# Scores of the later 128 queries as three float32r products of two-part operands, with the low part of g made by VectorE

## The reference

```python
q = (x @ Wq).reshape(b, t, h, e).transpose(0, 2, 1, 3)
k = (x @ Wk).reshape(b, t, h, e).transpose(0, 2, 1, 3)
v = (x @ Wv).reshape(b, t, h, e).transpose(0, 2, 1, 3)
q = q / math.sqrt(e)
dot = jnp.einsum('bhqe,bhke->bhqk', q, k)
dot = jnp.where(causal[None, None], dot, -jnp.inf)
att = jax.nn.softmax(dot, axis=-1)
out = jnp.einsum('bhqk,bhke->bhqe', att, v)
out = out.transpose(0, 2, 1, 3).reshape(b, t, h * e)
return out @ Wo + bo
```

## Time and profile before

| | us |
|---|---|
| median of three runs (2622.41 to 2632.78) | 2631.57 |
| span of the profiled execution, first to last instruction | 2620.5 |
| TensorE busy in it | 2267.1 (87%) |
| VectorE busy | 1887.6 (72%) |
| ScalarE busy | 1689.2 (64%) |
| GpSimd busy | 1152.6 (44%) |
| first head with an expert unit beside it, to last head of the attention | 1574 to 2464 |

### The profile page before, as it was taken

One profiled execution on the slowest core, in us unless ns is written; L12 is line 12 of the kernel. 1 busy time (PEld: TensorE's weight loads), 2 busy tenths in 40 slices (PEclk: granted clock), 3 DMA queues, 4 the chain that ended last, 5 costly groups with the idle time before them and its releaser, 6 DMA issues.

```text
span 2620.5 us, 58544 instructions
## 1 busy us (share of the span) xinstructions
PE 2267.1 (87%) x16671; PEld 2017.4 (77%) x16687; DVE 1887.6 (72%) x8724; ACT 1689.2 (64%) x5272; POOL 1152.6 (44%) x1358
## 2 busy tenths in 40 slices
PE   4999787676666699999999999999999999999954
PEld 3887665455555588888888889999999999999854
DVE  4887757544443488888888887787788888888622
ACT  3787653222222477777777778888888778888643
POOL 6444100788888202222222224444444666456553
PEclk9999989777777899999999999999999999999987
DMA  2333200344444521110101016556554777387687
GB/s 81 101 100 88 82 22 1 66 74 74 78 75 74 101 62 34 32 34 29 36 28 36 28 55 167 155 157 161 152 155 128 223 214 224 109 233 208 173 254 234
DMA packets 304256, 283.95 MB, mean 108 GB/s; under 512 B 33932, under 2 KB 252652, under 8 KB 303937
## 3 DMA queue, kind: packets, MB, share of 16 engines
q1 hardware_dynamic: 254144, 211.15, 29.4%
q0 software_dynamic: 46336, 61.16, 10.2%
q10 hardware_dynamic: 3456, 7.89, 1.0%
HBM read 185.85 MB, written 88.43 MB: 105 GB/s over the span
## 4 chain that ended last, share of the span: by engine, by line
PE 54%; DVE 18%; POOL 14%; issue 8%; DMA 3%; SPq 1%; ACT 1%; ACTq 0%; DVEq 0%; POOLq 0%
POOL hbuf L828 8%; PE bank L2040 6%; PE bank L2127 6%; PE bank L2113 5%; PE bank L2048 5%; PE bank L2080 4%; PE bank L2088 4%; POOL xe L820 4%; PE bank L2039 3%; PE bank L2062 3%; PE bank L2060 3%; PE bank L2061 3%; DVE pr_place L1558 2%; DVE nmax L1540 2%; DVE pr_place L1548 2%
## 5 line engine op out<-in xcount | busy, mean ns | idle before, releaser
L862 POOL DMA_INDIRECT spread_rows<-kb,pos x256 | 248.6, 971 | 595.4 <-ACT pr_place L1072 468.9
L877 POOL DMA_INDIRECT zbuf<-pc,kb x248 | 247.9, 1000 | 258.2 <-DVE pc L1720 207.5
L1070 ACT ACTIVATE pr_place<-bank,nmax 128x128 f32<-128x128 f32 x512 | 188.8, 369 | 201.5 <-DVE nmax L1540 198.5
L2040 PE MATMUL bank<-xT,gT 128*128 128x256 f32 x1024 | 306.7, 381 | 0.0
L2048 PE MATMUL bank<-ident,pr_place 128*128 128x128 f32 x1536 | 254.3, 275 | 43.4 <-DVE pr_place L1558 43.1
L2048 PEld LDWEIGHTS bank<-ident,pr_place 128*128 128x128 f32 x1536 | 189.6, 140 | 127.4 <-DVE pr_place L1551 62.4
L1558 DVE COPY pr_place<-bank 128x384 f32<-128x384 f32 x512 | 281.5, 550 | 1.1 <-PE bank L2048 1.0
L1539 DVE TENSOR_REDUCE nmax<-bank 128x1 f32<-128x128 f32 x512 | 144.1, 281 | 175.3 <-PE bank L2040 172.3
L2127 PE MATMUL bank<-wvo_part,x_part 128*128 128x512 f32 x768 | 269.0, 458 | 0.0
L1080 ACT ACTIVATE bank<-causal 128x384 f32<-128x384 f32 x512 | 253.4, 495 | 19.8 <-PE bank L2171 3.6
L2113 PE MATMUL bank<-x_part,wqk_part 128*128 128x256 f32 x1536 | 245.6, 296 | 1.2 <-DVE x_part L1665 1.2
(11 more groups left out here) (334 smaller groups left out, 6233.6 us busy)
## 6 DMA issues: line engine op xcount, KB each, us to landing
pa<-bundle SPq DMA_DIRECT2D x198, 321.0 KB
wu_more<-bundle SPq DMA_DIRECT2D x66, 321.0 KB
junk<-zbuf SPq DMA_DIRECT2D x32, 512.0 KB
kb<-spread_rows SPq DMA_DIRECT2D x248, 65.0 KB
xrow<-xr SPq DMA_DIRECT2D x32, 320.0 KB, 2.4
hbuf<-h SPq DMA_DIRECT2D x32, 256.0 KB, 3.1
hx<-hbuf SPq DMA_DIRECT2D x64, 128.0 KB
h3buf<-h SPq DMA_DIRECT2D x64, 128.0 KB
```

The source lines that it names most:

```text
L2040: pe.matmul(s2[:, P:3 * P], g[:, P:2 * P], xT3[:, p], start=False, stop=True, skip_group_check=True)\
```

## The change

For blocks n of at least SPLIT_FROM = 14 * 2 + 4 = 32, the L2040 product (float32, later 128 queries against 256 keys) becomes three float32r products, with g as two parts in the new buffer g_part and x as the two parts that x_part already holds. ACT's copy of a pair of heads is made in two: the later halves into g_part as the rounded part, the earlier halves into gT. DVE subtracts the rounded part from the bank to make the low part and signals g_low. PE waits for g_low before the three products, and before the gate's transposes and products that write the same bank. The earlier 128 queries' product (L2039) stays float32. The buffer xe moves to memory that layer 1 reuses, so that g_part fits.

```diff
--- before.py
+++ after.py
@@ -210,7 +210,6 @@
         cnt4 = sb("cnt4", [P, TG])
         idx = sb("idx", [P, 4, TG], U32)
 
-        xe = sb("xe", [P, 2, TG, ROW])
         xeT = sb("xeT", [P, TG * P])
         wup = sb("wup", [P, 2, FF])
         bup_n = sb("bup_n", [8, FF])
@@ -322,9 +321,11 @@
             wkn = sbe("wkn", [P, H1 * C])
             wvn = sbe("wvn", [P, H1 * C])
             won = sbe("won", [P, H1, C])
+            xe = sbe("xe", [P, 2, TG, ROW])
         wqk_part = [sb(f"wqk_part{k}", [P, H1, C], F32R) for k in range(2)]
         wvo_part = [sb(f"wvo_part{k}", [P, H1, C], F32R) for k in range(2)]
         x_part = [sb(f"x_part{k}", [P, 2, 2 * P], F32R) for k in range(2)]
+        g_part = sb("g_part", [P, 2, 2, 2, P], F32R)
 
         w_in = sem("w_in")
         consts = sem("consts")
@@ -411,6 +412,7 @@
         parts_split = sem("parts_split")
         g_mm = sem("g_mm")
         g_ready = sem("g_ready")
+        g_low = sem("g_low")
         vo_mm = sem("vo_mm")
         vo_ready = sem("vo_ready")
         s_mm = sem("s_mm")
@@ -431,6 +433,12 @@
 
         def there(u, count=NB * H1):
             return not isinstance(u, int) or 0 <= u < count
+
+        SPLIT_FROM = PORTS[0][1] * 2 + 4
+
+        def late_half(h):
+            v = bank[GBANK][:, :].rearrange("p (k q) -> p k q", k=2)[:, :, P:2 * P]
+            return v, g_part[:, h // 2 % 2]
 
         consts4 = sem("consts4")
         b1_ready = sem("b1_ready")
@@ -1137,7 +1145,13 @@
                             gates_turned(i - 1)
                         if h % 2 == 0 and n < NB:
                             act.wait_ge(g_mm, 4 * n + h // 2 + 1)
-                            act.activation(gT[:, h // 2 % 2], bank[GBANK][:, :], ACT.Copy).then_inc(g_ready, 1)
+                            if n < SPLIT_FROM:
+                                act.activation(gT[:, h // 2 % 2], bank[GBANK][:, :], ACT.Copy).then_inc(g_ready, 1)
+                            else:
+                                late, parts = late_half(h)
+                                act.activation(parts[:, 0], late, ACT.Copy)
+                                act.activation(gT[:, h // 2 % 2].rearrange("p (k q) -> p k q", k=2)[:, :, 0:P],
+                                               bank[GBANK][:, :].rearrange("p (k q) -> p k q", k=2)[:, :, 0:P], ACT.Copy).then_inc(g_ready, 1)
                         if h < 4 and n < NB:
                             act.wait_ge(vo_mm, 4 * n + h + 1)
                             act.activation(vo[:, p, h % 2, (h // 2) * 512:(h // 2 + 1) * 512], bank[VBANK][:, :], ACT.Copy)\
@@ -1765,6 +1779,10 @@
                         if there(u - N_LAG):
                             norm_rest(u - N_LAG, (h - N_LAG) % H1)
                         root_step()
+                        if h % 2 == 0 and SPLIT_FROM <= n < NB:
+                            late, parts = late_half(h)
+                            dve.wait_ge(g_ready, 4 * n + h // 2 + 1)
+                            dve.tensor_tensor(parts[:, 1], late, parts[:, 0].bitcast(F32), ALU.subtract).then_inc(g_low, 1)
                         if there(u - T_LAG):
                             turn(u - T_LAG, (h - T_LAG) % H1)
                         root_step()
@@ -2037,6 +2055,13 @@
                 pe.wait_ge(g_ready, 4 * n + h // 2 + 1)
                 pe.wait_ge(mask_set, u + 1)
                 pe.matmul(s2[:, 0:P], g[:, 0:P], xT3[:, p, 0:P], start=False, stop=True, skip_group_check=True)
+                if n >= SPLIT_FROM:
+                    pe.wait_ge(g_low, 4 * (n - SPLIT_FROM) + h // 2 + 1)
+                    for m, (a, b) in enumerate(PARTS):
+                        ins = pe.matmul(s2[:, P:3 * P], g_part[:, h // 2 % 2, b, h % 2], x_part[a][:, p], start=False, stop=(m == 2),
+                                        skip_group_check=True)
+                    ins.then_inc(s_mm, 1)
+                    return
                 pe.matmul(s2[:, P:3 * P], g[:, P:2 * P], xT3[:, p], start=False, stop=True, skip_group_check=True)\
                     .then_inc(s_mm, 1)
 
@@ -2098,9 +2123,13 @@
                             pe.wait_ge(parts_split, n + 3)
                         if (p, h) == (1, 1) and gated(i - 1):
                             pe.wait_ge(g_ready, min(4 * n + 1, 4 * NB))
+                            if n >= SPLIT_FROM:
+                                pe.wait_ge(g_low, min(4 * (n - SPLIT_FROM) + 1, 4 * (NB - SPLIT_FROM)))
                             gate_turn(i - 1)
                         if (p, h) == (1, 3) and gated(i - 1):
                             pe.wait_ge(g_ready, min(4 * n + 2, 4 * NB))
+                            if n >= SPLIT_FROM:
+                                pe.wait_ge(g_low, min(4 * (n - SPLIT_FROM) + 2, 4 * (NB - SPLIT_FROM)))
                             gate_products(i - 1)
                         if h % 2 == 0 and n < NB:
                             if (p, h) == (1, 2) and gated(i - 1):
```

## The result

The changed kernel took 2648.47 us (median of 6 runs, 2641.13 to 2652.78) against 2631.36 of the kernel before on the same chips (6 runs, 2622.41 to 2634.01): 1.0065 of it, 95% interval 1.005 to 1.0079. The forecast was 2629 with a range of 2611 to 2648. The time lies 0.5 us above the range, and inside what the second rival gave (2647 to 2650), which had a chance of 0.18.

The account below looks back on a forecast made before the run. PE was taken as the bound, DVE second: 4.9 us gained in the eight iterations up to 2015 us, 2.4 lost in the eight after, together -2.5 us from the 2631.6 median, giving 2629 us, range 2611 to 2648.

Parts of the forecast that it names:

- the second rival: Last eight iterations: PE waits for DVE held by POOL grow, clock drops; +15 to +18 us, 2647 to 2650, chance 0.18.
- The gain: Later queries' scores on PE: three products cost 0.355 us against 0.434, saving 0.079 us a head, 20.2 us over 256 heads.
- The quiet iterations: Eight iterations up to 2015 us, before POOL adds up results: 0.65 of 1.26 us given back each, 4.9 us gained.
- the three places: Slots (0,6), (1,0) with the gate, and (1,7), each with the next: PE waits for DVE, 0.35 to 0.85 us an iteration.
- (0,6): Slot of head 6 in an iteration's first block: the low part delays scores and turn, PE loses 0.30 us an iteration.
- The step that failed: Eight iterations after 2015 us, where POOL adds up results: 1.55 us back against 1.26 gained each, 2.4 us lost.
- wait up to 0.66 more: Gate's transposes in the last eight iterations, 0.66 us ahead of the scores: PE's added wait for the low part.
- the low part adds its 0.33 in full: Last eight iterations, where DVE is already late: each subtraction delays PE by its whole 0.33 us.
- Held up to 2.5 us: DVE's copies and multiplications inside SBUF: said to be held this long while POOL works.
- DVE takes over behind POOL's additions, slower: Title of the second rival: at turns and gate's transposes, each PE wait grows 0.4 to 1 us; chance 0.18.
- PE alone decides: Whole changed stretch: DVE's 122.7 us of waiting absorbs the low parts, at most 2 given back; 2611 to 2614, chance 0.24.
- The products are not cheaper: PE's three products take 0.43 us or more, so the gain is gone and losses stay; +13 to +18 us, chance 0.05.

Follow-up runs that it names:

- e3: Changed kernel with the three products kept but DVE's subtraction and its waits made only for the first two pairs; 2616.65 us, 0.995 of the kernel before.
- e1: Changed kernel with the split only in blocks 32 to 45, so the kernel before's program from iteration 24 on; 2629.13 us, 0.9997 of the kernel before.
- e4: Kernel before's single ACT copy and float32 product, plus DVE's subtraction that no product reads and PE's waits for it; 2649.95 us, 1.0073 of the kernel before.
- e5: Kernel before with POOL's result additions cut to 8 columns once; 2608.27 us, 0.9921 of the kernel before.
- e6: Changed kernel with POOL's result additions cut to 8 columns once; 2604.72 us, 0.9902 of the kernel before.
- e9: Kernel before with POOL's result additions spread, two per slot over four slots; 2619.69 us, 0.9962 of the kernel before.
- e11: Changed kernel with only head pairs (2,3) and (4,5) split and POOL's additions spread; 2615.78 us, 0.995 of the kernel before.
- e10: Changed kernel with POOL's result additions spread, two per slot over four slots; 2629.55 us, 1.0001 of the kernel before.
- e12: Changed kernel with DVE's subtraction moved right behind the maxima and POOL's additions spread; 2628.84 us, 1.0004 of the kernel before.

## Why the prediction was wrong

**The gain, right.** 0.434 less 0.355 us a head: the three products hold PE 0.36 us, and e3, where nothing is given back, shortens a quiet iteration by 1.19 us of the 1.26. The subtraction's 0.41 us was right as well, and so was ACT costed at nothing, nearly: in the changed profile DVE waits 2.6 us in all for its copies, and PE does not.

**The quiet iterations, right in kind and nearly in size.** Forecast: 0.65 of 1.26 given back at the three places, 0.6 gained. Measured: 0.50 gained, with 0.20 us given back at (0,6) and its turn where the rows gave 0.30. The eight together gave 2.0 us and not 4.9, mostly since the last of them was not alike: iteration 23 has six slots without an expert unit, and there PE waits already before the change (0.8 us in all, nearly all for DVE, and 1.8 with it); it went from 49.90 to 51.05 us. The forecast had read it as one of eight.

**The step that failed** is the one on the eight iterations after 2015 us: "That is 0.9 to 1.8 us back against 1.26". It gave 2.4 us lost. In the profiled executions, the stretch's gain of 127 x 0.079 = 10.0 us was lost and 20.4 us more: 30 us back in eight iterations, 3.8 each; by the medians (19 us more) it is 29. The terms, from the two profiles: PE's waits rose from 9.2 to 28.0 us (18.8); the clock's time at half speed rose from 3.4 to 13.7 us (5.1 lost); some 6 us are left. About 3 of these are in the waits themselves, since the list counts a wait from the modelled end of a record: the three products before the wait of 3.21 us start at 2190.85 and hold PE 0.70 us, so from there to 2194.92 it stood 3.37, 0.16 more than listed, and there are 29 such waits in place of 11. The other 3 stay unexplained. Against e1's trace in place of that before, the waits rise by 11.9 us and the clock's loss by 1.7; how much of the first account belongs to the change, and how much to the short execution that was profiled before it, single traces can't say.

What was wrong in that step is the size of the wait for the low part: "wait up to 0.66 more" for the gate's transposes, and "the low part adds its 0.33 in full" for the scores. Both took the lateness of DVE for the low part's own 0.33 us. But what stands ahead of the low part can be held beside POOL for 2.5 us, and PE now waits behind it: 2.22 us at one place, 7.0 us at the gate's transposes and 5.1 at the scores after iteration 23, against 0.6 and none in e1. Before the change the scores of a slot asked of DVE only what it had done two slots earlier; the low part asks for what it does in the slot just before. Lateness of a microsecond or two that these places did not feel came onto the path there. e4 agrees, with 8.4 us at the gate's transposes. What else its 20 us consist of, and whether each 0.33 us also counts at more than one place since DVE stays late over several slots, is argued and not shown.

Readings beneath that step were off too. The hold of 2.49 us was laid to the four additions in a row; POOL had done them at 2069.89, and the hold lasted to 2070.39, past the first of the next two. "Held up to 2.5 us" was 2.76 for L1548 in the same trace. And one profile, of an execution 11 us shorter than the median, was taken for the kernel. By busy time ACT and not DVE came second to PE over the two windows (738 us against 724), without consequence; and the three places of a quiet iteration add up to 0.35 to 0.80 us, not 0.85.

The fall of the clock after a long wait stood in the text, priced at 1.7 us each, but in the rival alone; the forecast of the mean held none. The whole executions have a granted clock of 0.937 (mean of six) where the kernel before has 0.940 (mean of the 22 in e1's rounds), which is some 7 us of lost clock more in 2640 us, an estimate. That is under half of the loss, and e4 lost 20 us at 0.939.

**The rivals.** "DVE takes over behind POOL's additions, slower" had the place and the time right, and its price of 15 to 18 us holds the measured 17. The way to that price was in part luck: it had four to six more falls where the trace has two more, the quiet iterations at 0 where they gained 2, and 8 us of more waiting where PE's waits rose by 12 to 19 (against e1's trace, against that of the kernel before). Its sign, more than two falls of the clock, does not tell the cases apart: e1 has three and is no slower, e3 has four and is 14 us faster. e5 and e6 carry its cause: take the additions away, and the change's loss is gone. The profile before held a hint: its three longest waits of PE (2.27, 1.84 and 1.66 us) are all behind DVE instructions held beside POOL. "PE alone decides" was the ceiling that e3 came near with 14 us. "The products are not cheaper" is excluded by e3.

**The signs named beforehand.** Right: three records in 0.36 us, the low part at 0.41, PE's wait at the turn between 15 and 25 us (though e1's trace has 17.9 without the change in the later blocks). Wrong: the waits were to be 0.1 to 0.4 us long, and the ones that count are 1 to 3; the first eight iterations were to shrink by 5 us and shrank by 2, the last eight to grow by 0 to 5 and grew by 20; DVE's wait for scores fell to 98 us and not to 70 or 80.

## What to carry to other kernels

Before work is moved to an engine with time to spare, look at how late that engine's slowest moments run and whether anybody waits for them now. Here the mean load said that there was room; what the forecast missed was the short distance between the new instruction and the one that needs it, with a hold of up to 2.5 us ahead of it. POOL's additions were such a hold for DVE's multiplications, and to break up their row gained 9 us in the kernel before, where the change lost 17. A part of a change can be worth more than the whole: with two of four pairs a quiet iteration gained 0.61 us, with four 0.50. And take more than one profile of the kernel before, or set its span against the runs: one execution showed half the waits of another.

## What was not expected of the hardware

- GpSimd's result additions cost the kernel before 21 us (e5), though GpSimd is busy 44% of the time (60% of the later stretch) and PE waits for none of them by name.
- Around or just behind the end of a single wait of PE of 2.0 to 3.3 us, in stretches where it is otherwise busy, there were in most cases 3.4 or 6.8 us at the lower level of the clock: 0.72 over 6 us before, 0.51 over 7 us in the change. In the change's profile waits of 2.05, 2.22 and 2.67 us had none. With the additions spread, e9 and e11 have no fall and no wait over 1.9 us; e10 and e12 have three each, behind waits of 2.0 to 2.3 us.
- One program's stretch of 450 us differed by 11 us between two executions of the same instructions (before and e1). The first has 6 holds of over 2 us and the second 12; what makes VectorE and GpSimd meet differently is not shown.
